# Query and key parts kept by element and then head and stored in four pieces; a result buffer for each chunk and a quarter on GpSimd in the last stage

## What is computed

```python
qkv = x @ c_attn_w.T + c_attn_b                  # q, k, v: 16 heads of 16
q_lat, k_lat, v_lat = q @ q2l_w.T + q2l_b, k @ kv2l_w.T + kv2l_b, v @ kv2l_w.T + kv2l_b
q_lat = q_lat * cos + rotate_half(q_lat) * sin   # the same for k_lat
q_for_k = q_lat @ wqk_w.T + wqk_b
att = softmax(causal(q_for_k @ k_lat.T * L ** -0.5))
x = layernorm(x + cproj(l2o(att @ v_lat)))
x = layernorm(x + experts(x))                    # top 2 of 8
```

## Time and profile before

| | us |
|---|---|
| median of 3 runs | 3118.36 (3117.6 to 3118.45) |
| the profiled execution, its own time | 3112.8 |
| its span in the trace | 3111.2 |
| PE busy | 2844.3 (91%) |
| DVE busy | 2273.6 (73%) |
| ACT busy | 1858.7 (60%) |
| POOL busy | 776.4 (25%) |

### The profile page before, as it was taken

The page is one execution under the profiler, slowest core; times in us unless marked ns, Lnnn a source line. Parts: engine busy times, 40 slices in busy tenths (PEclk is TensorE's granted clock), DMA queues, the critical chain, the costliest instruction groups (busy, mean ns, idle before and its releaser), DMA issues. The chain is left out here.

```text
span 3111.2 us, 50281 instructions
## 1 busy us (share of the span) xinstructions
PE 2844.3 (91%) x16538; PEld 1923.9 (62%) x16538; DVE 2273.6 (73%) x5659; ACT 1858.7 (60%) x3718; POOL 776.4 (25%) x701
## 2 busy tenths in 40 slices
PE   7888957999999999999999999999889997899990
PEld 5677744555555555555555555555367775799990
DVE  7999967888888888888888888888134543445443
ACT  4666632576667666666766676666535443546544
POOL 5777851010000001000110000010024444123220
PEclk9999986899999999999999999999989998899995
DMA  4666674242243234314332432340083220434316
GB/s 153 225 224 223 217 233 105 52 101 54 52 103 78 54 76 97 69 43 102 77 78 52 103 78 54 76 95 14 11 299 117 93 76 20 118 71 109 69 21 223
DMA packets 259647, 320.07 MB, mean 103 GB/s; under 512 B 70578, under 2 KB 157787, under 8 KB 258144
## 3 DMA queue, kind: packets, MB, share of 16 engines
q1 hardware_dynamic: 241760, 294.09, 33.4%
q0 software_dynamic: 17664, 23.19, 3.9%
HBM read 182.76 MB, written 143.95 MB: 105 GB/s over the span
## 5 line engine op out<-in xcount | busy, mean ns | idle before, releaser
L803 ACT ACTIVATE att_probs<-att_score_bank 128x512 f32<-128x512 f32 (+3 forms) x2560 | 1159.0, 551 | 608.5 <-PE att_score_bank L732 600.3
L840 DVE TENSOR_REDUCE att_partial_max<-att_max_bank 128x1 f32<-128x512 f32 x1536 | 1004.9, 687 | 124.3 <-PE att_max_bank L720 118.8
L720 PE MATMUL att_max_bank<-att_k_st,att_q_st 96*128 96x512 f32 (+3 forms) x2560 | 906.4, 389 | 31.8 <-DMA att_ident<-in_ident 20.9
L732 PE MATMUL att_score_bank<-att_q_st,att_k_st 98*128 98x512 f32 (+3 forms) x2560 | 924.5, 390 | 10.1 <-DMA att_q_st<-att_max_rows 7.6
L732 PEld LDWEIGHTS att_score_bank<-att_q_st,att_k_st 98*128 98x128 f32 x2560 | 481.8, 191 | 273.2 <-ACT att_probs L803 145.7
L720 PEld LDWEIGHTS att_max_bank<-att_k_st,att_q_st 96*128 96x128 f32 x2560 | 489.4, 193 | 244.7 <-DVE att_partial_max L840 100.7
L844 DVE CUSTOM_DVE_ANT_0 att_edge_sum<-att_max_bank,att_edge 128x128 f32<-128x128 f32 (+3 forms) x1024 | 482.0, 484 | 165.2 <-PE att_max_bank L720 164.7
L826 POOL TENSOR_SCALAR_AFFINE_SELECT att_probs<-att_probs 128x512 f32<-128x512 f32 x256 | 162.5, 635 | 1615.1 <-ACT att_probs L803 1615.1
L746 PE MATMUL att_acc_bank<-att_probs,att_v_st 128*32 128x512 f32 (+3 forms) x5120 | 544.2, 538 | 1.8 <-POOL att_probs L826 0.9
L210 POOL TENSOR_TENSOR proj_op_low<-proj_turned,proj_op_high 128x512 fp32r<-128x512 f32 x192 | 275.0, 1462 | 59.1 <-ACT proj_op_high L332 58.9
L746 PEld LDWEIGHTS att_acc_bank<-att_probs,att_v_st 128*32 128x32 f32 x5120 | 131.9, 109 | 245.2 <-issue 140.3
(11 more groups left out here) (221 smaller groups left out, 3887.3 us busy)
## 6 DMA issues: line engine op xcount, KB each, us to landing
qk_parts<-proj_parts SPq DMA_DIRECT2D x64, 1024.0 KB, 4.6
att_q_st<-qk_parts SPq DMA_DIRECT2D x192, 256.0 KB, 4.0
att_k_st<-qk_parts SPq DMA_DIRECT2D x192, 256.0 KB, 6.1
v_tokens<-proj_v_tok SPq DMA_DIRECT2D x64, 256.0 KB, 4.4
att_v_st<-v_tokens SPq DMA_DIRECT2D x64, 256.0 KB, 6.9
exp_w<-in_ew SPq DMA_DIRECT2D x16, 1024.0 KB, 8.9
dispatched<-mix_empty_rows SPq DMA_DIRECT2D x8, 1036.0 KB, 14.5
exp_rows<-dispatched SPq DMA_DIRECT2D x16, 518.0 KB, 5.5
```

The lines of the kernel that those rows point to most:

```text
L720: nc.tensor.matmul(max_ps[u % MAXB][:, 0:width], q_st[0:3 * L, n % QBUF, j, t * P:(t + 1) * P], k_st[0:3 * L, g % 2, kb, j, 0:width], star ...
L732: nc.tensor.matmul(score_ps[h % SCOREB][:, q0:CH], k_st[:, g % 2, kt // TT, j, (kt % TT) * P:(kt % TT + 1) * P], q_st[:, n % QBUF, j, q0:C ...
L803: nc.scalar.activation(probs[:, k % PROBS, j, q0:CH], score_ps[(HG * k + j) % SCOREB][:, q0:CH], ACT.Exp).then_inc(exped, 1)
L840: nc.vector.tensor_reduce(best, bank[:], AX.X, ALU.max).then_inc(unit_reduced, 1)
```

## The change

Two parts that have nothing to do with each other. First, the scratch tensor `qk_parts` in DRAM, which held 128 rows of 512 (head, then element) for each part, holds 32 elements by 4 heads by 512. The loads of `attend` then find, for one element, the four heads side by side: 8 KB in one piece where there were four pieces of 2 KB. The store can no longer be one transfer and becomes four, one for each head, from 32 partitions each; the counts on `parts_out` are multiplied by four. Second, `normalize` has 16 result buffers and no wait for one of them; ScalarE does three of the four instructions of a chunk, GpSimd the fourth, and SP waits for both.

```diff
                 for r in range(NU):
                     chunk, g = divmod(r, G)
                     sp.wait_ge(parts_done, units((seq, r), 1, 1 + 2))
-                    sp.dma_start(d["qk"][slot[g], chunk].rearrange("f p n -> p f n"),
-                                 parts[:, r % 2].bitcast(F32)).then_inc(parts_out[r % 2], 16)
+                    for j in range(HG):
+                        sp.dma_start(d["qk"][slot[g], chunk].rearrange("f l j n -> j l f n")[j],
+                                     parts[j * L:(j + 1) * L, r % 2].bitcast(F32)).then_inc(parts_out[r % 2], 16)
...
             def finish(c):
                 par = c[1] % 2
                 act.wait_ge(fin_q_ready, units(c, 1, 1 + OPS))
-                act.wait_ge(parts_out[par], units(c, 16, FREE, bufs=2))
+                act.wait_ge(parts_out[par], units(c, 16 * HG, FREE, bufs=2))
...
-        qk_src = d["qk"].rearrange("s c f (j p) n -> s c f p j n", p=L)
+        qk_src = d["qk"]
...
-        result = sb("result", [P, SUBS, TT, C])
+        result = sb("result", [P, NCH, TT, C])
...
             pool.memset(eps[:], EPS).then_inc(set_up, 1)
+            for ci in range(NCH):
+                pool.wait_ge(norm_ready, ci + 1)
+                nc.gpsimd.tensor_scalar(result[:, ci, MINE], z[:, ci, MINE], rstd[:, ci, MINE:MINE + 1],
+                                        shift[:, ci, MINE:MINE + 1], ALU.mult, ALU.add).then_inc(pool_result, 1)
...
             for ci in range(NCH):
-                sp.wait_ge(result_done, TT * (ci + 1))
-                sp.dma_start(out_dst[ci], result[:, ci % SUBS]).then_inc(stored[ci % SUBS], 16)
-            for i in range(SUBS):
-                sp.wait_ge(stored[i], 16 * NCH // SUBS)
+                sp.wait_ge(act_result, MINE * (ci + 1))
+                sp.wait_ge(pool_result, ci + 1)
+                sp.dma_start(out_dst[ci], result[:, ci]).then_inc(stored, 16)
+            sp.wait_ge(stored, 16 * NCH)
...
             def apply(ci):
                 act.wait_ge(norm_ready, ci + 1)
-                if ci >= SUBS:
-                    act.wait_ge(stored[ci % SUBS], 16 * (ci // SUBS))
-                for t in range(TT):
-                    nc.scalar.activation(result[:, ci % SUBS, t], z[:, ci, t], ACT.Identity, bias=shift[:, ci, t:t + 1],
-                                         scale=rstd[:, ci, t:t + 1]).then_inc(result_done, 1)
+                for t in range(MINE):
+                    nc.scalar.activation(result[:, ci, t], z[:, ci, t], ACT.Identity, bias=shift[:, ci, t:t + 1],
+                                         scale=rstd[:, ci, t:t + 1]).then_inc(act_result, 1)
...
-        "qk": scratch("qk_parts", (SLOTS, NC, 4, P, CH)),
+        "qk": scratch("qk_parts", (SLOTS, NC, 4, L, HG, CH)),
```

More of the change, by code:

```diff
@@ L237, in _ @@
             for i in range(2):
-                sp.wait_ge(parts_out[i], 16 * B * NU // 2 + FREE)
+                sp.wait_ge(parts_out[i], 16 * HG * B * NU // 2 + FREE)
                 sp.wait_ge(v_out[i], 16 * G * B * NC // 2 + FREE)
@@ L1728, in normalize @@
     NCH = B * NC
+    MINE = TT - 1
     with ExitStack() as ctx:
@@ L1747, in normalize @@
         norm_ready = sem("norm_ready")
-        result_done = sem("result_done")
-        stored = [sem(f"stored{i}") for i in range(SUBS)]
+        act_result = sem("act_result")
+        pool_result = sem("pool_result")
+        stored = sem("stored")
         block = ctx.enter_context(nc.Block())
```

## The result

The changed kernel takes **3145.44 us** (median of 4 runs, 3143.88 to 3146.23). The kernel before took 3118.4 beside it (3117.6 to 3118.84): ratio 1.0086, 95% interval 1.0069 to 1.0104. It is 27 us slower, where 12 us faster had been forecast and 3130 was the upper end.

A forecast was written before the change was run, and what follows sets the result against it. Attention was taken as bound by TensorE, the projection as near VectorE's and the DMA engines' limits. -18 (last stage) - 1 (attention) + 5 (drain) + 2 (chunk periods) = -12 us, so 3106.5 from 3118.4; range 3085 to 3130.

The forecast's parts named there:

- the last stage: Final layer norm: stores follow without gaps, 1.36 us each, instead of taking turns with ScalarE; -18 us.
- the rate of the stores: Projection: parts stores from 32 partitions move at 238 GB/s, 4.41 us of data, 1.65 us longer than before.
- The rival of pieces that are no slower: Projection: stores stay at 2.76 us and a chunk at 25.85; 3100 us in all, chance 0.15.
- the tie: Projection: the next lows' input comes at 10.5 us, just as GpSimd ends its third low, within 0.3 us.
- The mix of starved and unstarved chunks: Projection: some chunks starve VectorE, some not; 26.0 us a chunk, +2 us over 14 periods; chance 0.47.
- the other side: Projection: VectorE gets in and never starves; 24.9 us a chunk, 0.95 less; 3091 us in all, chance 0.20.
- The starved rival: Projection: VectorE starves behind GpSimd's lows in every chunk; 3129 us in all, chance 0.18.
- the price of the starved case: Projection: a starved chunk takes 27.6 us, 1.75 more than before; 14 x 1.75 = 24.5 us.
- the store behind the values: Projection, SP's queue: values' issues and the store after them slide by 1.1 us, under values data still moving.
- the drain: End of the projection, where nothing hides stores: three stores each 1.65 us longer, +5 us.
- attention: Loads with longer pieces: 3 us less waiting for small transfers or 1 us more; taken as -1 us.
- The projection: Whole projection stage: +2 us for the chunk periods and +5 for the drain, +7 in all.

The follow-up runs named there:

- e2: The kernel before with only the new last stage, layout and store as before: 3102.48 us, ratio 0.9933.
- e1: The kernel before with only the new layout and the four-piece store, last stage as before: 3162.96 us, ratio 1.0133.
- e13: The changed kernel with one of a chunk's four value pieces stored twice, the copy unread: 3140.82 us, ratio 1.0081.
- e7: The changed kernel with GpSimd's three lows ahead of the low part of x in every fourth step: 3127.85 us, ratio 1.0018.
- e14: The changed kernel with a chunk's values stored in one 1 MiB transfer instead of four: 3136.78 us, ratio 1.0067.
- e6: The changed kernel with four parts buffers instead of two: 3106.0 us, ratio 0.9952.
- e10: The changed kernel with all four value pieces of a chunk stored twice, the copies unread: 3211.01 us, ratio 1.0299.
- e11: The same kernel as e7 run once more for a second trace; the traced run took 3114.0 us.
- e5: The changed kernel with weight, bias and table rows reordered by element, then head, so one store from 128 partitions writes the new layout: 3100.46 us, ratio 0.9938.
- e12: e5 with four parts buffers instead of two: 3098.79 us, ratio 0.9937.
- e4: The kernel before, old layout, with its parts store in four pieces by head, 32 partitions each: 3161.49 us, ratio 1.0128.
- e3: The kernel before, old layout, with its parts store in four pieces by part, 128 partitions each: 3123.32 us, ratio 1.001.

## Why the prediction was wrong

**Right: the last stage.** -18 forecast, -17.4 in the trace, -17 in e2, and by the mechanism of the forecast: the stores follow one another, 1.42 us each where 1.36 were forecast, and end the span, while the results are ready ahead of them. VectorE's pace is the 1.85 us read in rows 12; GpSimd's new instruction takes 0.56 us, between its bounds of nothing and 1.25, and VectorE's L1813 beside it stays at 0.16.

**Right, with the size a little off: the rate of the stores.** I took 238 GB/s from the loads, 4.41 us of data; it is 224 to 228, 4.6 to 4.7 us for 1.05 MB, nearer the 4.8 estimated from the figure of 218 in the Trainium skill, "SBUF — State Buffer", section "Door 1: The DMA port swizzle". A store alone takes 6.1 us to ScalarE's start, 6.04 forecast. That holds although its four issues take SP 2.9 to 4.1 us from first to last, and not four times 0.37. The rival of pieces that are no slower is out.

**Wrong: the tie.** I set the gap between two starts of L320 at 3.67 + 4.41 = 8.1 us, as if values and store moved one after the other. It is 7.51 (219.70 to 227.21): in the transfers of the trace the values' first packets move at 217.9, while the store ahead of them has packets until 219.4, so the two overlap. So the input of the next lows comes at 9.8, GpSimd has its third low done at 10.4, and goes on: a tie read to 0.3 us was lost by 0.6. That is the pattern of seven chunks. In the other five the row has three lows only, and VectorE starves all the same, since with the late values it reaches L393 as the row begins; the forecast had no such case. The mix of starved and unstarved chunks, on which the forecast of 26.0 stood, did not come: 12 chunks of 12 have a block here, 11 of 12 in e1. e13 shows that the direction of the argument was right, since a gap of 8.9 us leaves no block over 2.9 us but the first. The 24.9 forecast for the other side looks confirmed by the 24.98 of e7, but that is in part luck: counted along the path of the forecast, the store is issued at 18.0 and not 19.0, and takes 7.0 and not 5.9 from there to L320. The starved rival, 3129, was the right case and had 0.18.

**Wrong: the price of the starved case**, 27.6 us against 28.8. The term that was too small is the time from issue to L320, 5.9 us on the path of the forecast (store issued at 21.7, L320 at 27.6), which is that of a store alone. The store on that path is the one with the values' transfers among its pieces, and it takes 6.95 and 6.98 us in the two chunks of the table, so 1.1 was missing in each. The engines' part of the path is 21.0 us in the chunk with the row of six, 0.7 less than forecast, and 23.0 in the one with late values, 1.3 more. I had written that the store behind the values slides along under their data. It slides by up to 2.5 us, and e14 puts the cost at some tenths of a us. In the sum the price is 12 us off: 36.6 measured for the periods against 14 x 1.75 = 24.5.

The late values go with TensorE's clock. TensorE waits until 242.6 for ScalarE's L321, 3.4 us, and then its granted clock is at the lower level (0.50, 1.2 GHz) up to 248, and the values' matmuls are late for VectorE by 1.63 us:

```profile
242.00:246.00 4.00, 3.41 (x8) 2.73 (x9) 4.00 (x5) 2.61 (x5) 2.35 (x2) 0.50 0.96 219
246.00:248.00 2.00, 2.00 (x10) 1.90 (x10) 0.75 (x2) 0.32 (x1) 2.00 (x2) 0.50 0.98 258
```

Over the 8 us ahead of L313 the granted clock is 0.61 to 0.79 in the five chunks with the block at L393 and 0.81 to 1.00 in the other seven. No run changes the clock alone, so how much of the 29.1 to 29.2 us of those five it makes stays open.

**Too small: the drain.** +5 forecast for three stores of 1.65 each. From ScalarE's high part of the last chunk's x (L313, 420.64 us) to the first load of attention it is 77.1 us, 68.7 before (L312, 383.62): +8.4. ScalarE waits up to 5.95 us for a store there, where rows 8 have 3.73, against the 1.65 more that was forecast; that the values' stores mix with the last parts stores is my reading, and no run separates it.

**Wrong in sign: attention.** -1 forecast; it takes 5.6 us more, and 2.0 to 6.5 more in the traces of e1, e6, e7, e10, e11, e13 and e14, all with this layout stored in pieces. TensorE's wait for the small transfer of rows 9 did not shrink but grew:

```profile
PE att_score_bank L733 <- DMA att_q_st<-att_max_rows: 8.7, 1, 8.7
```

The trace tells where the 5.6 us are. Counted from each kernel's start of attention, TensorE begins its 1000th matmul 1.6 us later than before and its 10400th 1.9 us later. The other 3.6 come within its last 96 matmuls, and there the granted clock differs. The last 15 us of attention's matmuls, before and then after:

```profile
2231.00:2246.00 15.00, 12.74 (x80) 5.01 (x72) 0.05 (x1) 8.29 (x21) 2.54 (x4) 0.99 0.01 2
```

```profile
2282.00:2297.00 15.00, 13.54 (x66) 4.87 (x65) 0.17 (x1) 5.90 (x17) 2.55 (x4) 0.63 0.00 1
```

The last 200 matmuls take 42.2 us before, 43.8 to 45.4 in the seven experiments without this pair of layout and pieces, and 43.8 to 48.6 in the kernels with it. Nothing here ties that clock to the layout. e5 has the same layout and the same 8 KB loads and takes 1798.0 (e12, with them too, 1799.5), e4 has the same slow stores and takes 1798.4; why all eight traces with both lie above these, if only by 0.5 us at the least, stays open.

**How the miss adds up.** The projection was forecast at +7 and came at +45.3. Of the 38.3 between them 22.4 are the starved case in place of the mix (14 x 1.6), 12.1 its price, 3.4 the drain and 0.4 the start. The +45.3 themselves are 35.4 for 12 chunks at 2.95, 1.2 for the one that follows them (25.35 against 24.10), 8.4 for the drain, and 0.4 at the start (45.4 by these rounded terms); with -17.4, +5.6 and -0.9 that is 32.6.

## What to carry to other kernels

In these runs a store from 32 or from 64 neighbouring partitions moved 212 to 228 GB/s, also when it was cut so that its pieces together covered all 128; if a layout in DRAM asks for that, turning the order of the rows in the weights gave the layout without the price. Where buffers are few, count a loop's period as round trips, engines' time plus time from issue to release, and take the release from a transfer with neighbours, since a lone one looks better than what the loop has. Two more buffers won back in the projection nearly what the faster store did (454.6 us in e6, 453.0 in e5). And where two engines' order hangs on which of two inputs comes first, price both sides as whole cases and forecast one of them, not their mean: the changed loop starved in 12 chunks of 12, and in 11 of 12 in its second trace.

## What was unexpected of the hardware

- Stores from 64 neighbouring partitions move 212 to 214 GB/s, no more than from 32 (224 to 228), where 128 move 350 to 380 (e3's stretch below, and rows 7).
- A kernel can be given more to store and be no slower: with 256 KB more in each of 16 chunks e13 has a ratio of 1.0081 (1.0057 to 1.0104), and the changed kernel 1.0086 (1.0069 to 1.0104).
- SP's issue of a piece grows along a row: 0.32, 0.32, 0.43 and 1.14 us for four pieces, 1.49 for the last of another four; from the first to the last of its four issues a store occupies SP for 2.9 to 4.1 us, where the single one of before takes 0.37 to 0.68. That what is queued makes the difference is my reading. The stretch of e3 that belongs to the first point:

```profile
206.00:208.00 2.00, 2.00 (x10) 1.65 (x9) 2.00 (x5) 1.60 (x3) 0.87 (x2) 1.00 0.97 350
```
